# Cross-attention logits as eight 32-channel products in one set, with ScalarE's other work gathered between tiles

## The chip, the cores and the metric

The kernel runs on one core of one Trainium2 chip. Its engines work side by side, each through its own list of instructions in order, and wait for one another on semaphores: TensorE (matrix products, PE in the rows), VectorE (DVE), ScalarE (ACT), GpSimd (POOL) and SyncE, which only starts transfers. The metric is the device time of one execution in microseconds (us); for the kernel before it is the median of three runs.

## The reference

A decoder layer on x of 4 sequences x 1024 tokens x 256 channels and a context of 4 x 77 x 256. Three blocks follow each other, each with a residual and a layer norm over the channels:

```
x = layernorm(x + self_attention(x))      # one head, sigmoid weights
x = layernorm(x + cross_attention(ctx, x))
x = layernorm(x + time_mixing(x))
```

The middle one is what the change is in. With 16 heads of 16 channels:

```
qh = split_heads(q @ wq_w.T + wq_b)       # q is x
kh = split_heads(k @ wk_w.T + wk_b)       # k, v are the context, 77 rows
vh = split_heads(v @ wv_w.T + wv_b)
logits = jnp.einsum('bhqd,bhkd->bhqk', qh, kh) * scale
attn = jax.nn.softmax(logits, axis=-1)
out = jnp.einsum('bhqk,bhkd->bhqd', attn, vh)
return merge_heads(out) @ dense_w.T + dense_b
```

## The kernel before

The 4096 tokens are 32 tiles of 128, taken in pairs: NJ = 16 pairs, pair i holding tiles 2i and 2i+1. Each engine's program is written out by hand as a list of calls in Python, and that list is the order in which it works; a call waits for the semaphores of the work that it needs (`w.wait_ge`). Self-attention fills the first 300 us. Then comes the loop `for s in range(NJ)`, sixteen steps of cross-attention, and after it the time mixing, which begins with `mixes(0)` on VectorE.

A tile's way in the loop, with the names of the calls and of what they write:

1. `x1` (TensorE) transposes the normed tokens of a pair; `x1_hi` (ScalarE) and `x1_lo` (VectorE) split them into a high and a low part; `query` (TensorE) makes the queries, and ScalarE's `query` copies them to `xq` with the bias. Channels lie on the 128 partitions, in two halves e = 0, 1 of 128 channels (8 heads each).
2. `cross_scores(t, e)` (TensorE, L1303) makes the logits of 8 heads of tile t. The keys lie in `kb` as blocks: in the 64 partitions of four heads, four blocks of 77 columns, each zero but in the rows of its own head. One product over 64 partitions with 308 columns so gives four heads at once, and two such products, of the upper and the lower 64 partitions, make the half set e. They are plain float32, which TensorE does in two passes, each with its weight load. The four results of a tile go to four banks of PSUM (`big` and `ring` in the rows). A half set waits until the exponentials of the same half of tile t-1 are read out.
3. `maxima(t, e)` (VectorE, L906, `neg_mx`) takes the minima of the negated logits, per bank; `exponentials(t, e)` (ScalarE, L400, `p_sb`) then makes the softmax numerators, one instruction per head, four per bank.
4. `fold_weights(t)` (GpSimd, L658, `fold`) adds the two halves of each head's 78 columns, `sums(t)` (VectorE, L912, `sm`) and `reciprocals(t)` (L919, `rc`) make the reciprocal sums, `normalise(t)` (GpSimd, L663) multiplies them in. `fold` is one buffer, `sm` and `rc` are two.
5. `weights_t(t, c)` (TensorE, L1319) turns the weights, in three parts c; `weights_body` (VectorE, L926, `pT`) copies two of them out of PSUM, `weights_tail` (ScalarE) the third.
6. `mixed(i)` (TensorE, L1336) multiplies with the values for a pair, 32 columns of the array at a time; `mixed_hi` (ScalarE) and `mixed_lo` (VectorE, `oT_lo`) split the result; `dense(i)` is the output product; `crossed(i)` (VectorE, L939) adds the residual, `stats2` (L944, L949), `deviation2` (GpSimd) and `norm2` (ScalarE) are the layer norm.

Steps overlap: step s makes the logits of pair s, turns the weights of tiles 2s-3 and 2s-2, mixes pair s-2, does the dense product of pair s-3 and the norm of pair s-4. GpSimd's list in a step is `fold_weights(2s-1)`, `residual2(s)`, `normalise(2s-1)`, `fold_weights(2s)`, `normalise(2s)`, `deviation2(s-3)`. On VectorE `sums(2s)` is nearly the last of the step, and the ordering of the calls around it is what the rows and lists below show.

Ahead of the loop the first half set of tile 0 is written before the last `attend` of self-attention, and `maxima(0, 0)` before `attended(NG - 1)`, which frees the banks of the second half.

## Time and profile before

| | us |
|---|---|
| median of 3 runs | 595.7 (595.64 to 595.77) |
| the profiled execution | 593.07 |
| its span, first to last instruction | 591.1 |
| TensorE busy in the span | 544.1 (92%) |
| VectorE busy | 439.9 (74%) |
| ScalarE busy | 377.5 (64%) |
| GpSimd busy | 339.1 (57%) |
| exponentials (L400) out of `big`, 384 | 89.8, 359 ns each |
| logits' products (L1303) into `big`, 192 passes | 51.1, 482 ns each |

The times of the runs are of whole executions, the span is that of the instructions alone. Busy times are sums of durations, and the matmuls' ends are modelled: where they are pipelined, durations overlap, so that what a product costs is read from the starts of it and of the next. The granted clock of TensorE was 0.985 of 2.4 GHz over the span, and 1.00 in each 20 us from 340 to 480 us. A row of the timeline merges like instructions in a row (x4: four of them); the number in brackets is the time in which the engine had nothing to do before them, and behind the arrow is what ended it.

### The profile page before, as it was taken

The page shows a single profiled execution, that of the slowest core. Times are in us where ns is not written, and L with a number is a line of the kernel's source. Part 1 is how long each engine was busy: PE and PEld are TensorE (multiplying, and loading weights), DVE is VectorE, ACT ScalarE, POOL GpSimd, SP SyncE. Part 2 cuts the span into 40 slices and gives each one's busy share as a digit, 9 for nine tenths or more (in the row PEclk, how much of TensorE's full clock was granted, in tenths as well). Part 3 has the DMA queues.
Part 4 walks back from the last instruction along what each step waited for, and adds up shares of the span by engine and source line. Part 5 has one row for each costly group of instructions (what it writes and reads, how often), then busy time and mean ns, then how long its engine had stood idle before and what let it go on. Part 6 is the DMA issues. An engine that isn't in the chain of part 4 may idle for free.

```text
span 591.1 us, 11142 instructions
## 1 busy us (share of the span) xinstructions
PE 544.1 (92%) x3952; PEld 453.6 (77%) x3952; DVE 439.9 (74%) x1027; ACT 377.5 (64%) x1013; POOL 339.1 (57%) x382
## 2 busy tenths in 40 slices
PE   3879999999999999999978999999999986899993
PEld 2668988898998989987765677667767655799993
DVE  2975577666666777666537889889989878799995
ACT  1254344444344454443368989999899885899974
POOL 2645245253435334150427887898898883169996
PEclk9999999999999999999988999999999998999997
DMA  6210101010103002110000000000000000001113
GB/s 182 71 55 19 54 19 54 19 53 19 41 21 101 1 1 72 34 54 2 0 2 0 2 2 2 0 3 1 1 3 1 2 2 0 1 19 55 54 54 108
DMA packets 18351, 17.53 MB, mean 30 GB/s; under 512 B 1835, under 2 KB 18296, under 8 KB 18296
## 3 DMA queue, kind: packets, MB, share of 16 engines
q1 hardware_dynamic: 18024, 16.57, 9.1%
q8 instruction: 31, 0.51, 0.4%
q10 hardware_dynamic: 272, 0.26, 0.1%
q14 instruction: 24, 0.20, 0.1%
HBM read 12.63 MB, written 4.19 MB: 28 GB/s over the span
## 4 chain that ended last, share of the span: by engine, by line
PE 47%; POOL 20%; DVE 16%; ACT 8%; issue 6%; DMA 2%; SPq 1%; POOLq 0%; DVEq 0%; ACTq 0%
PE ring L218 20%; PE big L218 19%; POOL p_sb L663 9%; POOL fold L658 6%; DVE big L970 3%; ACT p_sb L400 2%; POOL xs L650 2%; PE ring L1209 2%; PE big L1303 2%; POOL rs L674 1%; DVE xmT_lo L788 1%; PE ring L1319 1%; DVE y L996 1%; DMA bo<-in_bo 1%; DVE st L817 1%
## 5 line engine op out<-in xcount | busy, mean ns | idle before, releaser
L788 DVE TENSOR_TENSOR aT_lo<-a_sb,aT_hi 128x512 fp32r<-128x512 f32 x64 | 45.8, 717 | 78.2 <-ACT aT_hi L324 78.2
L400 ACT ACTIVATE p_sb<-big,neg_mx 128x77 f32<-128x77 f32 x384 | 89.8, 359 | 13.3 <-DVE neg_mx L906 13.2
L663 POOL TENSOR_TENSOR p_sb<-p_sb,rc 128x1248 f32<-128x1248 f32 x32 | 72.8, 2277 | 23.3 <-DVE rc L919 23.3
L218 PE MATMUL big<-vv_hi,aT_hi 128*128 128x256 f32 x256 | 72.7, 284 | 4.0 <-DVE xs L852 4.0
L357 ACT ACTIVATE a_sb<-ring,nlogs 128x512 f32<-128x512 f32 x64 | 43.5, 680 | 49.5 <-PE ring L218 49.5
L218 PE MATMUL big<-vv_hi,aT_lo 128*128 128x256 f32 x256 | 72.5, 283 | 0.0
L218 PE MATMUL big<-vv_lo,aT_hi 128*128 128x256 f32 x256 | 72.4, 283 | 0.0
L1319 PE MATMUL ring<-ident,p_sb 128*128 128x128 f32 (+1 forms) x384 | 55.5, 280 | 8.4 <-DVE pT L926 7.8
L1319 PEld LDWEIGHTS ring<-ident,p_sb 128*128 128x128 f32 (+1 forms) x384 | 40.2, 130 | 29.3 <-issue 20.5
L1303 PE MATMUL big<-kb,xq 64*128 64x308 f32 x192 | 51.1, 482 | 5.9 <-ACT p_sb L400 4.5
L218 PEld LDWEIGHTS big<-vv_hi,aT_hi 128*128 128x128 f32 x256 | 48.8, 191 | 9.1 <-issue 6.8
L218 PE MATMUL ring<-qkT_hi 128*128 128x512 f32 x128 | 51.6, 403 | 0.0
L218 PEld LDWEIGHTS big<-vv_lo,aT_hi 128*128 128x128 f32 x256 | 48.8, 191 | 2.1
L587 POOL TENSOR_TENSOR rs<-mv,consts 128x2 f32<-128x2 f32 x32 | 12.5, 389 | 65.9 <-DVE mv L820 65.9
L218 PE MATMUL ring<-qkT_lo,qkT_hi 128*128 128x512 f32 x128 | 50.2, 392 | 0.0
L658 POOL TENSOR_TENSOR fold<-p_sb 128x624 f32<-128x624 f32 x32 | 48.7, 1523 | 2.3 <-ACT p_sb L400 2.3
L218 PE MATMUL ring<-qkT_hi,qkT_lo 128*128 128x512 f32 x128 | 49.9, 390 | 0.0
L218 PEld LDWEIGHTS big<-vv_hi,aT_lo 128*128 128x128 f32 x256 | 48.8, 191 | 0.0
L324 ACT ACTIVATE xT_hi<-xraw 128x512 fp32r<-128x512 f32 x16 | 10.1, 630 | 56.2 <-PE big L218 50.0
L906 DVE TENSOR_REDUCE neg_mx<-big 128x4 f32<-128x308 f32 x96 | 41.3, 459 | 4.9 <-PE big L1303 3.6
L926 DVE COPY pT<-ring 128x512 f32<-128x512 f32 x64 | 43.3, 680 | 1.7 <-PE ring L1319 1.7
L597 POOL TENSOR_TENSOR vv_lo<-v_sb,vv_hi 128x512 fp32r<-128x512 f32 x16 | 21.0, 1315 | 40.5 <-ACT vv_hi L324 40.5
(172 smaller groups left out, 1748.8 us busy)
## 6 DMA issues: line engine op xcount, KB each, us to landing
xraw<-in_xT SPq DMA_DIRECT2D x16, 256.0 KB, 2.8
xs<-in_x SPq DMA_DIRECT2D x8, 512.0 KB, 3.8
out_y<-y SPq DMA_DIRECT2D x16, 256.0 KB, 2.1
cT<-in_cT SPq DMA_DIRECT2D x1, 308.0 KB
wraw<-in_wqT ACTq DMA_DIRECT2D x1, 256.0 KB, 3.9
wraw<-in_wkT SPq DMA_DIRECT2D x1, 256.0 KB, 4.3
wv_raw<-in_wv SPq DMA_DIRECT2D x1, 256.0 KB, 5.7
wo_ls<-in_woT SPq DMA_DIRECT2D x1, 256.0 KB, 5.8
```

Of the source, the lines that this page charges most:

```text
L218: mm = pe.matmul(out, s_, m_, start=first and k == 0 and q == 0, stop=last and k == n - 1 and q == 2, skip_group_check=not check)
L357: act.activation(a_sb[:, i % NAR], st_bank[i % 2], ACT.Sigmoid, bias=nlogs[:, 0:1], scale=1.0 / 16).then_inc(st_act.sem, 1)
L400: ex = act.activation(weights(t)[:, HG * g + h, 0:SC], logits[g][:, h * SC:(h + 1) * SC], ACT.Exp, bias=neg_mx[:, t % 2, HG * g + h:HG * g ...
L597: pool.tensor_tensor(lo, tiles(v_sb[:, i % 2]), f(hi), ALU.subtract).then_inc(v_pool.sem, 1)
L658: pool.tensor_tensor(fold[:].rearrange("p (h k) -> p h k", k=FO), p[:, :, 0:FO], p[:, :, FO:2 * FO], ALU.add).then_inc(fo_pool.sem, 1)
L663: pool.tensor_tensor(weights(t), weights(t), rc[:, t % 2].rearrange("p (h o) -> p h o", o=1) .to_broadcast([P, H, SP]), ALU.mult).then_inc ...
L788: return dve.tensor_tensor(lo, whole, f(hi), ALU.subtract)
L906: dve.tensor_reduce(neg_mx[:, t % 2, HG * g:HG * (g + 1)], logits[g][:, 0:LW].rearrange("p (h k) -> p h k", k=SC), AX, ALU.min)\
L926: dve.tensor_copy(pT[:, t // 2 % 2, c, :, (t % 2) * P:(t % 2 + 1) * P], tiles(tp_bank[(3 * t + c) % 2], NH)).then_inc(tp_dve.sem, 1)
L970: dve.scalar_tensor_tensor(out=xm_bank[m][:, k * D:(k + 1) * D], in0=ty_bank(i)[:, k * D:(k + 1) * D], scalar=mu[:, m, k:k + 1], in1=carry ...
L1303: mm = pe.matmul(logits[2 * e + r][:, 0:LW], xq[half, i % 2, e * D + u * P:e * D + (u + 1) * P], kb[half, b, e], start=True, stop=True)
L1319: mm = pe.transpose(tp_bank[n % 2][0:rows, g * P:(g + 1) * P], p_sb[:, t % NP, c0:c0 + rows], ident[:])
```

## The change

The keys' blocks get smaller: two heads in the 32 partitions of two heads (KH = 2, KW = 154 columns). `cross_scores(t)` makes all sixteen heads of a tile in one set: for each half e of the channels, four products over 32 partitions with 154 columns, into the four banks, each bank getting two heads of either half. The set waits for all exponentials of tile t-1. `maxima(t)` and `exponentials(t)` do all four banks of a tile in a row. The first half set ahead of the last `attend` goes. The lists of ScalarE, VectorE and TensorE are written anew, with the other calls between the tiles. `query(s + 2)` at the end of a step becomes `query(s + 1)` in its middle.

The diff, cut:

```diff
@@ -29,6 +29,8 @@
+KH = 2
+KW = KH * SC
@@ -143,11 +146,11 @@
-            mask_k = tensor(ph, "mask_k", [P, HG])
+            mask_k = tensor(ph, "mask_k", [P, KH])
-            kb = tensor(ph, "kb", [P, B, KC, LW])
+            kb = tensor(ph, "kb", [P, B, KC, KW])
@@ -381,7 +384,7 @@
                 def query(i):
                     w.wait_ge(*xq_pe.at(i))
                     if i >= 2:
-                        w.wait_ge(*xs_pe.at(2 * (2 * (i - 2) + 1) + 1))
+                        w.wait_ge(*xs_pe.at(2 * (i - 2) + 1))
                     for e in range(KC):
                         cut = slice(e * D, (e + 1) * D)
                         copy(xq[:, i % 2, cut], x_bank[:, cut], bias=bqcol[:, e:e + 1]).then_inc(xq_act.sem, 1)
@@ -389,16 +392,17 @@
                 def first_exponential():
                     act.activation(spare[:], minus4[:, 0:1], ACT.Exp).then_inc(table.sem, 1)
-                def exponentials(t, e):
+                def exponentials(t):
                     if t >= NP:
                         w.wait_ge(*tp_pe.at(3 * (t - NP) + 2))
                     else:
                         w.wait_ge(*st_pe.at(NS - 1))
-                    for g in (2 * e, 2 * e + 1):
-                        w.wait_ge(*mx_dve.at(4 * t + g))
+                    for n in range(4):
+                        w.wait_ge(*mx_dve.at(4 * t + n))
                         for h in range(HG):
-                            ex = act.activation(weights(t)[:, HG * g + h, 0:SC], logits[g][:, h * SC:(h + 1) * SC], ACT.Exp,
-                                                bias=neg_mx[:, t % 2, HG * g + h:HG * g + h + 1], scale=-1.0)
+                            ex = act.activation(weights(t)[:, h // KH * (H // 2) + KH * n + h % KH, 0:SC],
+                                                logits[n][:, h * SC:(h + 1) * SC], ACT.Exp,
+                                                bias=neg_mx[:, t % 2, HG * n + h:HG * n + h + 1], scale=-1.0)
                         ex.then_inc(ex_act.sem, 1)
                 def weights_tail(t):
@@ -415,9 +419,9 @@
-                def norm2(i):
+                def norm2(i, ts=(0, 1)):
-                    for t in range(2):
+                    for t in ts:
@@ -516,24 +520,24 @@
                 first_exponential()
                 x1_hi(2)
                 for s in range(NJ):
-                    exponentials(2 * s, 0)
+                    exponentials(2 * s)
                     if s >= 2:
                         weights_tail(2 * s - 3)
-                    exponentials(2 * s, 1)
-                    if s and s + 2 < NJ:
-                        x1_hi(s + 2)
+                    if s and s + 1 < NJ:
+                        query(s + 1)
                     if s == 1:
                         norm1_last()
                     if s >= 4:
-                        norm2(s - 4)
-                    exponentials(2 * s + 1, 0)
+                        norm2(s - 4, (0,))
+                    exponentials(2 * s + 1)
+                    if s and s + 2 < NJ:
+                        x1_hi(s + 2)
                     if s >= 2:
                         mixed_hi(s - 2)
-                    exponentials(2 * s + 1, 1)
+                    if s >= 4:
+                        norm2(s - 4, (1,))
                     if s >= 1:
                         weights_tail(2 * s - 2)
-                    if s + 2 < NJ:
-                        query(s + 2)
                 first_sigmoid()
                 weights_tail(NT - 3)
                 carried(0)
@@ -640,9 +644,9 @@
-                                           .to_broadcast([P, HG, SC]),
+                                           .to_broadcast([P, KH, SC]),
-                                           .to_broadcast([P, HG, SC]), ALU.mult).then_inc(kb_pool.sem, 1)
+                                           .to_broadcast([P, KH, SC]), ALU.mult).then_inc(kb_pool.sem, 1)
@@ -898,13 +902,13 @@
                     w.wait_ge(*tx_act.at(i))
                     low_part(*hi_lo(x1T, i % 2), x_bank).then_inc(tx_dve.sem, 1)
-                def maxima(t, e):
-                    w.wait_ge(*xs_pe.at(2 * t + e))
+                def maxima(t):
+                    w.wait_ge(*xs_pe.at(t))
                     if t >= 2:
                         w.wait_ge(*ex_act.at(4 * (t - 2) + 3))
-                    for g in (2 * e, 2 * e + 1):
-                        dve.tensor_reduce(neg_mx[:, t % 2, HG * g:HG * (g + 1)],
-                                          logits[g][:, 0:LW].rearrange("p (h k) -> p h k", k=SC), AX, ALU.min)\
+                    for n in range(4):
+                        dve.tensor_reduce(neg_mx[:, t % 2, HG * n:HG * (n + 1)],
+                                          logits[n][:, 0:LW].rearrange("p (h k) -> p h k", k=SC), AX, ALU.min)\
                             .then_inc(mx_dve.sem, 1)
                 def sums(t):
@@ -1087,37 +1091,30 @@
                         value_blocks(4)
                         value_blocks(5)
                 x1_lo(2)
-                maxima(0, 0)
                 attended(NG - 1)
-                maxima(0, 1)
                 for s in range(NJ):
-                    if s:
-                        maxima(2 * s, 0)
+                    maxima(2 * s)
                     if s >= 2:
                         weights_body(2 * s - 3, 0)
+                        weights_body(2 * s - 3, 1)
                     if s >= 3:
                         crossed(s - 3)
-                    if s:
-                        maxima(2 * s, 1)
-                    if s >= 2:
-                        weights_body(2 * s - 3, 1)
                     if s >= 1:
                         sums(2 * s - 1)
                         reciprocals(2 * s - 1)
-                    maxima(2 * s + 1, 0)
+                    maxima(2 * s + 1)
+                    if s == 0:
+                        stats1(NG - 1)
                     if s >= 1:
                         weights_body(2 * s - 2, 0)
+                    sums(2 * s)
+                    reciprocals(2 * s)
+                    if s >= 1:
+                        weights_body(2 * s - 2, 1)
                     if s and s + 2 < NJ:
                         x1_lo(s + 2)
-                    maxima(2 * s + 1, 1)
-                    if s == 0:
-                        stats1(NG - 1)
                     if s >= 2:
                         mixed_lo(s - 2)
-                    if s >= 1:
-                        weights_body(2 * s - 2, 1)
-                    sums(2 * s)
-                    reciprocals(2 * s)
                     if s >= 3:
                         stats2(s - 3)
                 weights_body(NT - 3, 0)
@@ -1287,21 +1284,21 @@
                                            [hi_lo(x1T, i % 2, slice(k * D, (k + 1) * D)) for k in range(KC)])
                     mm.then_inc(xq_pe.sem, 1)
-                def cross_scores(t, e):
+                def cross_scores(t):
                     i, u = divmod(t, 2)
                     b = t // TB
                     w.wait_ge(*xq_act.at(i))
                     w.wait_ge(*kb_pool.at(b))
                     if t:
-                        w.wait_ge(*ex_act.at(4 * (t - 1) + 2 * e + 1))
-                    elif e:
+                        w.wait_ge(*ex_act.at(4 * (t - 1) + 3))
+                    else:
+                        w.wait_ge(*vb_dve.at(5))
                         w.wait_ge(*ln1a_dve.at(NG - 1))
-                    else:
-                        w.wait_ge(*vb_dve.at(5))
-                    for r in range(2):
-                        half = slice(64 * r, 64 * (r + 1))
-                        mm = pe.matmul(logits[2 * e + r][:, 0:LW], xq[half, i % 2, e * D + u * P:e * D + (u + 1) * P],
-                                       kb[half, b, e], start=True, stop=True)
+                    for e in range(KC):
+                        for n in range(4):
+                            own = slice(32 * n, 32 * (n + 1))
+                            mm = pe.matmul(logits[n][:, e * KW:(e + 1) * KW], xq[own, i % 2, e * D + u * P:e * D + (u + 1) * P],
+                                           kb[own, b, e], start=True, stop=True)
                     mm.then_inc(xs_pe.sem, 1)
                 def weights_t(t, c):
@@ -1451,32 +1448,28 @@
                 attend(NS - 3)
                 attend(NS - 2)
                 x1(2)
-                cross_scores(0, 0)
                 attend(NS - 1)
                 for s in range(NJ):
-                    if s:
-                        cross_scores(2 * s, 0)
+                    cross_scores(2 * s)
+                    if s >= 2:
+                        weights_t(2 * s - 3, 0)
+                        weights_t(2 * s - 3, 1)
                     if s >= 3:
                         dense(s - 3)
+                    if s and s + 1 < NJ:
+                        query(s + 1)
                     if s >= 2:
-                        weights_t(2 * s - 3, 0)
-                    cross_scores(2 * s, 1)
+                        weights_t(2 * s - 3, 2)
+                    cross_scores(2 * s + 1)
+                    if s >= 1:
+                        weights_t(2 * s - 2, 0)
+                        weights_t(2 * s - 2, 1)
                     if s >= 2:
-                        weights_t(2 * s - 3, 1)
-                        weights_t(2 * s - 3, 2)
+                        mixed(s - 2)
                     if s and s + 2 < NJ:
                         x1(s + 2)
-                    cross_scores(2 * s + 1, 0)
                     if s >= 1:
-                        weights_t(2 * s - 2, 0)
-                    if s >= 2:
-                        mixed(s - 2)
-                    cross_scores(2 * s + 1, 1)
-                    if s >= 1:
-                        weights_t(2 * s - 2, 1)
                         weights_t(2 * s - 2, 2)
-                    if s + 2 < NJ:
-                        query(s + 2)
                 dense(NJ - 3)
                 for c in range(3):
                     weights_t(NT - 3, c)
@@ -1505,7 +1498,7 @@
     row = np.arange(P)
-    mask_k = ((row[:, None] // DH) % HG == np.arange(HG)[None, :]).astype(np.float32) * np.float32(-DH ** -0.5)
+    mask_k = ((row[:, None] // DH) % KH == np.arange(KH)[None, :]).astype(np.float32) * np.float32(-DH ** -0.5)
     flat = np.arange(3 * P)
     sel = ((flat[None, :] % SP == np.arange(SC)[:, None]) & (flat[None, :] < PG)).astype(np.float32)
     head = flat.reshape(3, P).T // SP
```

VectorE's list around `sums(2s)` in a middle step, before (`x1T_lo` is `x1_lo`, `oT_lo` is `mixed_lo`, `pT` are the copies of `weights_body`, `sm` the sums; the first row is `weights_body(2s-2, 0)`):

```order
L926 COPY pT<-ring 128x4x128
L788 TENSOR_TENSOR x1T_lo<-ring,x1T_hi 128x512
L906 TENSOR_REDUCE neg_mx<-big 128x4 x2
L788 TENSOR_TENSOR oT_lo<-ring,oT_hi 128x512
L926 COPY pT<-ring 128x4x128
L912 TENSOR_REDUCE sm<-fold 128x16
L919 RECIPROCAL rc<-sm 128x16
L944 BN_STATS st<-xs 128x6 x2
L949 BN_AGGR mv<-st 128x2 x2
```

And now:

```order
L930 COPY pT<-ring 128x4x128
L916 TENSOR_REDUCE sm<-fold 128x16
L923 RECIPROCAL rc<-sm 128x16
L930 COPY pT<-ring 128x4x128
L792 TENSOR_TENSOR x1T_lo<-ring,x1T_hi 128x512
L792 TENSOR_TENSOR oT_lo<-ring,oT_hi 128x512
L948 BN_STATS st<-xs 128x6 x2
L953 BN_AGGR mv<-st 128x2 x2
```

The low part of x1, that of the mixed values and the second copy have moved from ahead of the sums of tile 2s to behind their reciprocal. The minima of tile 2s+1 are all ahead of the first copy now.

ScalarE's list over one step, before (`p_sb` are exponentials, eight heads of a half in the first two rows):

```order
L400 ACTIVATE p_sb<-big,neg_mx 128x77 x4
L400 ACTIVATE p_sb<-ring,neg_mx 128x77 x4
L324 ACTIVATE pT<-ring 56x4x128
L400 ACTIVATE p_sb<-big,neg_mx 128x77 x8
L324 ACTIVATE x1T_hi<-ring 128x512
L324 ACTIVATE xs<-xs,nb,rs 128x256 x2
L400 ACTIVATE p_sb<-big,neg_mx 128x77 x4
L400 ACTIVATE p_sb<-ring,neg_mx 128x77 x4
L324 ACTIVATE oT_hi<-ring 128x512
L400 ACTIVATE p_sb<-big,neg_mx 128x77 x8
```

And now:

```order
L403 ACTIVATE p_sb<-big,neg_mx 128x77 x4
L403 ACTIVATE p_sb<-ring,neg_mx 128x77 x4
L403 ACTIVATE p_sb<-big,neg_mx 128x77 x8
L327 ACTIVATE pT<-ring 56x4x128
L327 ACTIVATE xq<-ring,bqcol 128x256 x2
L327 ACTIVATE xs<-xs,nb,rs 128x256
L403 ACTIVATE p_sb<-big,neg_mx 128x77 x4
L403 ACTIVATE p_sb<-ring,neg_mx 128x77 x4
L403 ACTIVATE p_sb<-big,neg_mx 128x77 x8
L327 ACTIVATE x1T_hi<-ring 128x512
L327 ACTIVATE oT_hi<-ring 128x512
```

Sixteen exponentials stand in a row now, and the copies of the weights' tail, the queries, x1 and the mixed values and the halves of `norm2` (`xs`) are behind them.

## Rows read from the trace of the kernel before

**Rows 1.** Timelines at the ends of the stage: start us, us, engine, line, operation

```profile
310.27 1.39 DVE L857 BATCH_NORM_STATS2 stl<-xs 128x6 f32<-128x256 f32 x4
...
313.57 2.27 POOL L663 TENSOR_TENSOR p_sb<-p_sb,rc 128x1248 f32<-128x1248 f32 x1
...
344.81 2.28 POOL L663 TENSOR_TENSOR p_sb<-p_sb,rc 128x1248 f32<-128x1248 f32 x1 [1.72 <-DVE rc L919]
...
479.71 0.39 PE L218 MATMUL ring<-wx_hi,oT_hi 128*128 128x256 f32 x1 [1.11 <-DVE oT_lo L788]
...
481.33 2.28 POOL L663 TENSOR_TENSOR p_sb<-p_sb,rc 128x1248 f32<-128x1248 f32 x1 [1.25 <-DVE rc L919]
...
488.80 1.67 DVE L970 SCALAR_TENSOR_TENSOR big<-ring,mu,carry 128x256 f32<-128x256 f32 x4
```

**Rows 2.** Waits of all engines, 360 to 460 us: total us, times, longest

```profile
POOL p_sb L663 <- DVE rc L919: 12.5, 9, 1.5
...
DVE sm L912 <- POOL fold L658: 8.5, 9, 1.0
...
ACT p_sb L400 <- DVE neg_mx L906: 5.3, 8, 0.7
```

**Rows 3.** Timeline of TensorE, one step

```profile
400.47 0.28 PE L218 MATMUL ring<-x1T_hi,wx_lo 128*128 128x256 f32 x1
400.68 0.52 PE L1303 MATMUL big<-kb,xq 64*128 64x308 f32 x1
...
401.04 0.42 PE L1303 MATMUL big<-kb,xq 64*128 64x308 f32 x1
...
401.39 0.39 PE L218 MATMUL ring<-wx_hi,oT_hi 128*128 128x256 f32 x1
...
407.08 1.93 PE L1336 MATMUL ring<-pT,vb 128*32 128x256 f32 x32
```

**Rows 4.** Timeline of TensorE, two half sets in a row

```profile
305.44 0.42 PE L1303 MATMUL ring<-kb,xq 64*128 64x308 f32 x1
...
305.70 0.42 PE L1303 MATMUL ring<-kb,xq 64*128 64x308 f32 x1
```

**Rows 5.** Timeline of ScalarE, the same step

```profile
399.75 1.84 ACT L400 ACTIVATE p_sb<-big,neg_mx 128x77 f32<-128x77 f32 x8
401.41 0.67 ACT L324 ACTIVATE pT<-ring 56x512 f32<-56x512 f32 x1
```

**Rows 6.** Timeline of VectorE, the same step

```profile
401.15 0.79 DVE L912 TENSOR_REDUCE sm<-fold 128x16 f32<-128x624 f32 x1
401.98 0.25 DVE L919 RECIPROCAL rc<-sm 128x16 f32<-128x16 f32 x1
402.15 0.69 DVE L944 BATCH_NORM_STATS2 st<-xs 128x6 f32<-128x256 f32 x2
...
402.97 0.46 DVE L906 TENSOR_REDUCE neg_mx<-big 128x4 f32<-128x308 f32 x1
...
403.73 0.68 DVE L926 COPY pT<-ring 128x512 f32<-128x512 f32 x1
404.33 0.68 DVE L939 TENSOR_TENSOR xs<-ring,xs 128x512 f32<-128x512 f32 x1
404.93 0.85 DVE L906 TENSOR_REDUCE neg_mx<-big 128x4 f32<-128x308 f32 x2
...
407.32 0.80 DVE L912 TENSOR_REDUCE sm<-fold 128x16 f32<-128x624 f32 x1 [0.95 <-POOL fold L658]
```

**Rows 7.** Timeline of GpSimd, the same step

```profile
402.31 2.28 POOL L663 TENSOR_TENSOR p_sb<-p_sb,rc 128x1248 f32<-128x1248 f32 x1 [1.48 <-DVE rc L919]
...
405.78 1.51 POOL L658 TENSOR_TENSOR fold<-p_sb 128x624 f32<-128x624 f32 x1
...
408.50 2.27 POOL L663 TENSOR_TENSOR p_sb<-p_sb,rc 128x1248 f32<-128x1248 f32 x1
410.73 1.53 POOL L658 TENSOR_TENSOR fold<-p_sb 128x624 f32<-128x624 f32 x1
```

More of the change, by code:

```diff
@@ L1295, in cross_scores @@
                     if t:
-                        w.wait_ge(*ex_act.at(4 * (t - 1) + 2 * e + 1))
-                    elif e:
-                        w.wait_ge(*ln1a_dve.at(NG - 1))
+                        w.wait_ge(*ex_act.at(4 * (t - 1) + 3))
                     else:
                         w.wait_ge(*vb_dve.at(5))
-                    for r in range(2):
-                        half = slice(64 * r, 64 * (r + 1))
-                        mm = pe.matmul(logits[2 * e + r][:, 0:LW], xq[half, i % 2, e * D + u * P:e * D + (u + 1) * P],
-                                       kb[half, b, e], start=True, stop=True)
+                        w.wait_ge(*ln1a_dve.at(NG - 1))
+                    for e in range(KC):
[3 more added lines that the diff above has]
+                                           kb[own, b, e], start=True, stop=True)
                     mm.then_inc(xs_pe.sem, 1)
```

## The prediction

> **What bounds the kernel now.** I read the views in this order: the page's busy shares, the waits of the cross-attention steps, the timelines of one step on each engine, and the rows at its two ends. The kernel has three parts: self-attention to 301 us, sixteen steps of cross-attention (two tiles of 128 tokens a step) to about 481 us, and the mixing behind it. Only the middle one is changed, so its step is the thing to price. The normalising product on GpSimd at step 3 starts at 344.81 and at step 15 at 481.33 [rows 1]: 12 steps in 136.52 us, 11.38 us a step.
>
> Over 100 us of it TensorE shows no wait for another engine; GpSimd waits 12.5 us for VectorE's reciprocals, VectorE 8.5 us for GpSimd's folds, ScalarE 5.3 us for the minima [rows 2]. So TensorE sets the step, but narrowly: ScalarE, idle for 5% of it, has some 10.8 us of work in 11.38, and VectorE and GpSimd wait for each other. A TensorE that is relieved can give back 0.6 us a step at most, and only if the other loops turn faster than 11.38.
>
> **Price of the products on TensorE.** A half set now (two 64-row products, two passes each) starts 0.21 us behind the multiply before it, where a plain multiply takes 0.12: 0.09 of drain. Its passes start at 400.68 and 401.04, the next work at 401.39, so 0.36 and 0.35 us [rows 3]. Where two half sets follow each other the spacing is 0.26 (305.44 to 305.70) [rows 4]; so a pass streams 308 columns in 0.26, and only the first load (0.10) and the drain (0.09) lie open. With the first load of the work behind, also open (0.10), a half set costs 0.09+0.36+0.35+0.10 = 0.90 us, and a step has four: 3.6.
>
> The new set has eight products of 154 columns, two passes each: 16 multiplies in four groups of four. A group streams for 0.26/2 = 0.13 if its four run together. The trace has no four row groups together, but it has four column groups: 32 multiplies of 256 columns took 1.93 us [rows 3], where one by one they would take 32 x 0.26 x 256/308 = 6.9. So I take four together: 0.09+0.10+4x0.13+0.09+0.10 = 0.90 for the set. The lower bound is 0.7, if switching costs nothing; the upper is one by one, 16 x 0.13 + 0.38 = 2.5. TensorE then has two sets instead of four half sets, 1.8 us less a step, about 9.5 us of work.
>
> The Trainium skill, TensorE: Matmul & The Clock Gate, Part 3 (packing small matmuls), says that a weight load overlaps a running multiply only where their row groups differ. By that rule each group would show its load, and the set would take 4x0.23+0.28 = 1.2 us, an estimate. The trace disagrees: the same row groups follow at 0.26, with no load between [rows 4].
>
> **The loop over the logits.** With one set, the products of a tile wait for all sixteen exponentials of the tile before. Eight exponentials take 399.75 to 401.41 [rows 5], 0.21 each, so 3.32 for sixteen; then about 0.2 until the last is written, 0.8 for the set and 0.5 for the first minimum: 4.8 us a tile, 9.6 a step. What waits there is ScalarE's exponentials, and the copies of earlier tiles gathered behind them fill most of that time. With 10.8 us of work ScalarE stays under 11.38 too. With the set at 2.5 us this loop is 6.5 a tile, 13 a step, and decides.
>
> **The loop over VectorE and GpSimd.** Here the order matters. Three pieces of VectorE's step used to stand ahead of the sums of tile 2s (the low part of x1, the low part of the mixed values, the second copy of the turned weights), and hid the fold that the sums wait for. Now they stand behind the sums. The way from the sums of tile 2s-1 to those of 2s leads over GpSimd, where the fold of 2s stands behind the normalising of 2s-1. Step by step, start to start [rows 6, 7]:
> sums 2s-1 0.83 (401.15 to 401.98); reciprocal to normalising 0.33 (401.98 to 402.31); normalising 2.23 (408.50 to 410.73); fold until the sums start 1.54 (405.78 to 407.32); sums 2s 0.83; reciprocal 0.17; then the copy, x1's low part and the mixed low part, three of 128x512 out of PSUM at 0.60 (403.73 to 404.33); statistics 0.82 (402.15 to 402.97); four minima 1.52 (402.97 to 403.73 for two); two copies and the residual sum 1.80. Together 11.87 us, and it closes on the sums of tile 2s+1. In the order before, the three pieces of 0.60 were not in it: 10.07 us, below TensorE's 11.38. Nothing in this loop is TensorE's, so its gain is worth nothing here: the stall moves from TensorE to VectorE, which is late by 0.5 us a step. For ScalarE I cost the new places at nothing: norm2 in two parts and the query's copy stand in the time between tiles, where it would wait; without that cover they are the same instructions and come to the same 10.8 us.
>
> **The sum.** Steps 3 to 15: eleven links at 11.87 and the last, which has no x1, at 11.27: 141.84 against 136.52, +5.3. Steps 0 to 3 took 31.24 us (313.57 to 344.81), 10.4 a link: the first ones hang on GpSimd's own work and stay, the third lacks the statistics, 11.87-0.82 = 11.05, about as now; I take them at -0.2 together, an estimate. Start: the first tile is no longer half done ahead of the last attend. Its sixteen exponentials stand behind one another (+8x0.21 = 1.66), two more minima stand ahead of the first statistics (+0.76), and the attend comes 0.8 earlier since no half set is ahead of it: the statistics at 310.27 [rows 1] come 1.6 later, and the first normalising (313.57) with them. End: dense(13) starts at 479.71, held up by the mixed low part, and mixes(0) at 488.80 [rows 1], 9.1 later. That low part now stands behind the sums of tile 30 and the copy. Normalising at step 15 comes at 481.33+6.7 = 488.0, so the sums at 486.9, the copy at 487.9, the low part at 488.5 and dense at 489.2. From there 8.3 us (the 9.1 less the 0.8 in which the next low part stood behind the last sums): mixes(0) at 497.5, +8.7, of which 2.0 are the new exit. Everything behind hangs on mixes(0), and I carry the shift whole.
>
> Smaller changes: the block keys have half the columns, work of GpSimd hidden under self-attention, at nothing; one mask load is shorter. TensorE has gaps of at most 0.6 us in a step now, which I take as too short to lower its clock; it was granted in full all through these steps before.
>
> The profiled execution took 593.07 us for a span of 591.1; the three timed ones have a median of 595.7. The shift is a difference of schedules, so I add it to the median: 595.7 + 8.7 = 604.4 us.
>
> **The rivals.**
> First, the four don't run together, only two or one. For it: no row shows four row groups. Against it: four column groups do, and two row groups do now, or a pass of both would take 0.52 and not 0.26 [rows 4]. In pairs the set is 1.4 us, the logits loop 10.8, hidden still, with some +1 at the start. One by one (2.5 us) the logits loop of 13.0 a step decides: 12 x (13.0-11.38) = 19, with 2 at the start and 2 at the end 23: 618 us. Half-way prices give 608 to 615.
> Second, faster: the VectorE loop does not bind because its pieces are shorter together than start-to-start spacings say, or the folds come earlier. It decides if the loop falls by more than 0.5 us, to under 11.38. Then ScalarE's 10.8 us are the step: 12 x 0.6 = 7.2 less, 1.6 more at the start: 590 us. For it: TensorE's 1.8 us are real, and ScalarE's work is under 11.38. Against: each term of 11.87 is a row, and the engines run in order.
> Third, the two effects meet and the time stays at 595.7: a loop near 11.3, with start and end shifts given back. Nothing speaks for it but that errors can cancel.
> Fourth, the change doesn't do what it says on the logits: TensorE's wait for sixteen exponentials lengthens, as ScalarE's gathered copies wait in turn for TensorE (the copy of x1 and of the weights' tail are produced behind the products). That gives another 0.3 to 0.5 us a step, 609 us.
>
> **How the numbers follow.** Forecast (loop at 11.6 to 12.0, 601 to 607 us) 0.62. Products or copies slower (607 to 618) 0.19. Faster 0.12. No change 0.03, and a weak slow-down of 1 to 5 us 0.04. A change under 0.2%, 1.2 us, can't be told from none. Slower then is 0.62+0.19+0.04 = 0.85, the same 0.03, faster 0.12. For 8 in 10 the range has to hold the forecast and most of the slower cases: 598 to 611.
>
> **What the profile will show.** If right: GpSimd's normalising of tile 2s starts every 11.9 us; VectorE waits for a fold once a step, about 1.2 us, and not for the other; the gap of the logits' multiplies between groups is 0.13; TensorE waits some 2 us a step for exponentials and copies; the first normalising at 315.2. Wrong on the products: groups at 0.26 or more. Wrong on the loop: VectorE's copy behind the sums not followed at once, or steps under 11.4.

## The result and the profile after

The changed kernel took 605.8 us (median of four, 604.35 to 607.62) against 595.7 (595.13 to 595.77): 1.73% slower, ratio 1.0173 [1.0137, 1.0209]. The forecast was 604.4. The profiled execution of after took 607.07 us for a span of 604.8, so it is one of its longer ones: its span is 13.7 us over that of before (591.1), the medians lie 10.1 apart. What follows explains the 13.7 of the two profiled executions.

The rows below are from the changed kernel's timelines: GpSimd's normalising of tile 2s at steps 0, 3 and 15, and VectorE's mixes(0). Columns are start, duration, engine, line, operation, idle time before and what ended it:

```profile
315.54 2.27 POOL L667 TENSOR_TENSOR p_sb<-p_sb,rc 128x1248 f32<-128x1248 f32 x1
...
348.77 2.28 POOL L667 TENSOR_TENSOR p_sb<-p_sb,rc 128x1248 f32<-128x1248 f32 x1 [1.20 <-DVE rc L923]
...
490.87 2.28 POOL L667 TENSOR_TENSOR p_sb<-p_sb,rc 128x1248 f32<-128x1248 f32 x1 [1.21 <-DVE rc L923]
```
```profile
500.81 1.67 DVE L974 SCALAR_TENSOR_TENSOR big<-ring,mu,carry 128x256 f32<-128x256 f32 x4
```

Against [rows 1] that is +1.97 at the start, +2.0 in steps 0 to 3 (33.23 against 31.24), +5.6 in steps 3 to 15 (142.10 against 136.52, eleven links of 11.89 and one of 11.29), +2.5 from there to mixes(0) (9.94 against 7.47), and +1.7 behind it (104.0 against 102.3 to the end of the span).

The longest waits between 360 and 460 us (engine and line, what it waits for, total, times, longest):

```profile
POOL p_sb L667 <- DVE rc L923: 13.4, 17, 1.2
ACT p_sb L403 <- DVE neg_mx L910: 12.6, 9, 1.4
PE big L1300 <- ACT p_sb L403: 11.1, 17, 1.1
DVE sm L916 <- POOL fold L662: 9.5, 9, 1.1
```

In [rows 2] TensorE waited for nobody. Now it waits for the exponentials before every set (17 times in 8.4 steps), ScalarE's waits have more than doubled (5.3 to 12.6) and VectorE waits for one fold a step, 1.1 us. Everybody waits for somebody: a closed way through several engines, a loop, sets the step. Its course is on the chain of waits, one step from 402 us (start, duration, what; most rows left out):

```profile
402.95 0.29 issue
...
403.27 2.28 POOL p_sb L667
405.55 1.48 POOL fold L662
...
407.06 0.82 DVE sm L916
...
408.15 0.54 DVE pT L930
408.69 0.59 DVE x1T_lo L792
409.29 0.60 DVE oT_lo L792
409.88 0.39 DVE st L948 x2
...
411.19 0.66 POOL rs L678
...
412.12 1.49 POOL fold L662
413.61 1.23 POOL xs L654
```

The first half is the loop of the forecast: normalising, fold, sums, and behind the sums the three pieces that used to hide the fold. Behind the statistics the forecast went on over VectorE (minima, copies, sums); the chain goes over GpSimd's deviation, fold and residual instead. That branch is 0.29 us shorter than mine: for so long GpSimd stands ready for the normalising (the first row) until the reciprocals are there. The timelines show what the normalising really waits for:

```profile
402.12 0.79 DVE L916 TENSOR_REDUCE sm<-fold 128x16 f32<-128x624 f32 x1
...
402.94 0.25 DVE L923 RECIPROCAL rc<-sm 128x16 f32<-128x16 f32 x1
...
403.27 2.28 POOL L667 TENSOR_TENSOR p_sb<-p_sb,rc 128x1248 f32<-128x1248 f32 x1 [0.33 <-DVE rc L923]
```

From the sums at 407.06 to the reciprocals of the next step VectorE has no hole, so in the changed kernel the branch over VectorE ends last, as forecast.

The set of products, on TensorE's timeline:

```profile
402.91 0.39 PE L1300 MATMUL big<-kb,xq 32*128 32x154 f32 x1 [1.03 <-ACT p_sb L403]
...
403.15 0.29 PE L1300 MATMUL ring<-kb,xq 32*128 32x154 f32 x1
...
403.41 0.29 PE L1300 MATMUL ring<-kb,xq 32*128 32x154 f32 x1
...
403.64 1.09 PE L1316 MATMUL ring<-ident,p_sb 128*128 128x128 f32 x8
```

Four groups of four (the third starts at 403.28), 0.24 and then 0.13 apart: the four products do run together, and 154 columns take half of the 0.26 of [rows 4]. From its first product to the next work the set takes 0.73 us. My 0.90 also holds 0.09 of drain ahead of the set, which here lies in the wait, and 0.10 for the first load of the next work; between the same two starts it has 0.10+0.52+0.09 = 0.71. So the price was right within 0.02. The weight loads of the second group start at 403.01, in the same four row groups that multiply from 402.91 on. The Trainium skill (TensorE: Matmul & The Clock Gate, Part 3) states that a load overlaps a running product only where their row groups differ; with this the trace again disagrees. The same section of the Trainium skill also lets a load go ahead of running products when it goes to a background weight buffer, which would allow what the trace shows; no run here shows the buffer itself.

TensorE's clock, by stretches (length, busy time of PE, PEld, DVE, ACT, POOL, granted clock, DMA). After:

```profile
300.00:320.00 20.00, 8.93 (x84) 7.63 (x82) 10.07 (x26) 11.31 (x51) 9.43 (x13) 0.74 0.00 0
320.00:340.00 20.00, 16.05 (x164) 12.93 (x165) 14.40 (x31) 17.27 (x65) 16.09 (x10) 0.83 0.01 2
340.00:480.00 140.00, 118.98 (x1378) 92.33 (x1376) 119.48 (x270) 123.72 (x477) 115.62 (x104) 1.00 0.01 2
...
500.00:520.00 20.00, 14.30 (x109) 12.61 (x110) 14.13 (x33) 11.27 (x24) 2.92 (x11) 0.83 0.00 1
```

And before:

```profile
300.00:320.00 20.00, 14.51 (x80) 9.70 (x79) 12.02 (x31) 14.62 (x58) 11.39 (x14) 0.83 0.00 0
320.00:340.00 20.00, 19.25 (x168) 13.38 (x170) 16.68 (x36) 18.53 (x77) 16.66 (x11) 1.00 0.01 2
...
500.00:520.00 20.00, 18.06 (x162) 16.22 (x162) 14.02 (x30) 18.05 (x41) 2.85 (x8) 1.00 0.00 1
```

In the steady steps the clock is full in both, as forecast. At the ends it is lower than before: 0.74 against 0.83 in the first stretch, 0.83 against 1.00 in the second and behind 500 us. Ahead of the second and third set TensorE waits 4.2 us for sixteen exponentials, and those sets run at the lower of the two levels, 1.2 GHz (granted clock 0.50, groups 0.25 apart):

```profile
309.21 0.62 PE L1300 MATMUL big<-kb,xq 32*128 32x154 f32 x1 [4.19 <-ACT p_sb L403]
...
314.81 0.62 PE L1300 MATMUL big<-kb,xq 32*128 32x154 f32 x1 [4.20 <-ACT p_sb L403]
```

### The profile page after: what moved, and what is told of

Its sections match the earlier page's. It is cut to its first block, busy times and chain, and to the rows that moved or that the text cites. A ratio compares the mean times of both kernels' runs of the same rounds, so it can differ in the third digit from the quotient of the medians.

```text
span 604.8 us, 11640 instructions
## 1 busy us (share of the span) xinstructions
PE 528.4 (87%) x4208; PEld 455.6 (75%) x4208; DVE 440.4 (73%) x1027; ACT 376.7 (62%) x1013; POOL 338.2 (56%) x382
## 4 chain that ended last, share of the span: by engine, by line
PE 43%; DVE 23%; POOL 19%; ACT 6%; issue 5%; DMA 2%; SPq 1%; POOLq 0%; DVEq 0%; ACTq 0%
PE big L221 18%; PE ring L221 18%; POOL fold L662 7%; POOL p_sb L667 6%; DVE big L974 3%; POOL xs L654 3%; PE ring L1206 2%; ACT p_sb L403 2%; DVE sm L916 2%; DVE oT_lo L792 1%; DVE pT L930 1%; DVE xmT_lo L792 1%; DVE y L1000 1%; DMA bo<-in_bo 1%; POOL rs L678 1%
## 5 line engine op out<-in xcount | busy, mean ns | idle before, releaser
L403 ACT ACTIVATE p_sb<-big,neg_mx 128x77 f32<-128x77 f32 x384 | 92.1, 390 | 28.5 <-DVE neg_mx L910 28.5
L1316 PE MATMUL ring<-ident,p_sb 128*128 128x128 f32 (+1 forms) x384 | 58.9, 287 | 12.3 <-DVE pT L930 7.6
L1316 PEld LDWEIGHTS ring<-ident,p_sb 128*128 128x128 f32 (+1 forms) x384 | 41.9, 134 | 23.3 <-DVE pT L930 8.8
L1300 PE MATMUL big<-kb,xq 32*128 32x154 f32 x384 | 28.3, 338 | 31.7 <-ACT p_sb L403 30.2
L1300 PEld LDWEIGHTS big<-kb,xq 32*128 32x128 f32 x384 | 20.4, 201 | 40.1 <-ACT p_sb L403 35.3
L327 ACT ACTIVATE xT_hi<-xraw 128x512 fp32r<-128x512 f32 x16 | 10.1, 630 | 55.7 <-PE big L221 50.0
```

Source lines behind the costliest of these rows:

```text
L403: ex = act.activation(weights(t)[:, h // KH * (H // 2) + KH * n + h % KH, 0:SC], logits[n][:, h * SC:(h + 1) * SC], ACT.Exp, bias=neg_mx[: ...
L1300: mm = pe.matmul(logits[n][:, e * KW:(e + 1) * KW], xq[own, i % 2, e * D + u * P:e * D + (u + 1) * P], kb[own, b, e], start=True, stop=True)
L1316: mm = pe.transpose(tp_bank[n % 2][0:rows, g * P:(g + 1) * P], p_sb[:, t % NP, c0:c0 + rows], ident[:])
```

## The experiments

Every ratio is to the kernel before on the same chip, in the same rounds (its medians there were 593 to 595). "Step" is the spacing of GpSimd's normalising in the steady part, 11.89 in the changed kernel. A time that is read from a single trace also holds what came before the loop: the first set starts at 304.21 in the changed kernel, but at 305.81 in experiment 1, 306.08 in 6, 304.00 in 3 and 303.77 to 304.04 in 5, 7, 8 and 9, though none of their edits touches the self-attention ahead of it.

**1. One term out of the loop.** On VectorE, `stats2(s - 3)` goes from the end of the step to its middle:

```
+                    if s >= 3:
+                        stats2(s - 3)
                     maxima(2 * s + 1)
...
                     if s >= 2:
                         mixed_lo(s - 2)
-                    if s >= 3:
-                        stats2(s - 3)
```

> The changed kernel with one call moved on VectorE: the statistics of pair s-3 stand ahead of the minima of tile 2s+1, where VectorE waits 0.6 us for the products anyway, and no longer between the sums of tile 2s and those of 2s+1. Theory A (the loop over VectorE and GpSimd, 11.87 us, sets the step): the loop loses the 0.82 us of the statistics and is 11.05, so steps of 11.05 to 11.2 us, 12 of them, and some 9 us less than the changed kernel: about 597. Rival B (the loop over the logits, with its wait for sixteen exponentials on TensorE, sets the step): nothing changes, 605 to 606, steps of 11.9.

Measured: step 11.17, ratio 1.0055 [1.0038, 1.0073], 597.5 us. Moving 0.82 us of work, without removing any, gives back two thirds of the slow-down (1.18 of 1.73%). So the step is set by something that goes through VectorE's statistics, as the forecast's loop does; experiment 5 shows a second loop that also does. What decides next is GpSimd's own chain, whose only hole is a wait for reciprocals:

```profile
400.42 2.28 POOL p_sb L667
402.69 1.48 POOL fold L662
404.18 1.17 issue
...
405.38 2.28 POOL p_sb L667
```

**2. Wide products in the new order.** Each set as four products of 64 channels again (and the exponentials' heads in the order that goes with them):

```
-KH = 2
+KH = HG
...
-                        for n in range(4):
-                            own = slice(32 * n, 32 * (n + 1))
-                            mm = pe.matmul(logits[n][:, e * KW:(e + 1) * KW], xq[own, i % 2, e * D + u * P:e * D + (u + 1) * P],
-                                           kb[own, b, e], start=True, stop=True)
+                        for r in range(2):
+                            half = slice(64 * r, 64 * (r + 1))
+                            mm = pe.matmul(logits[2 * e + r][:, 0:LW], xq[half, i % 2, e * D + u * P:e * D + (u + 1) * P],
+                                           kb[half, b, e], start=True, stop=True)
```

> The schedule of the changed kernel with the products of before: four of 64 partitions and 308 columns in the one set of a tile. A set then takes about 0.10+4x0.26+0.18 = 1.3 us on TensorE in place of 0.8. Theory A: TensorE has slack in every step of the new schedule, the step stays at 11.9, only the first steps, where each tile waits for its products, get longer: +1 to +2 us over the changed kernel, 607. Rival B (TensorE or the logits loop sets the step): 32 sets x 0.5 = +16 us, 621.

Measured: step 12.15, ratio 1.0310 [1.0288, 1.0332], 613.2 us: between the two. In this order the narrow products save 0.26 a step, not 1: 3.1 us of the 7.4 between the medians. By the traces another 1.5 lie in the first normalising (317.02), 0.9 in steps 0 to 3 and 1.0 in the exit. The chain of a steady step tells why it is so little: it is now a loop over the logits, and it goes through VectorE's pieces, which my 9.6 us for that loop had left out:

```profile
400.35 0.69 DVE x1T_lo L792
...
402.43 0.47 DVE neg_mx L910
...
402.93 2.81 ACT p_sb L403 x13
...
406.54 0.52 PE big L1300
...
407.90 0.49 DVE neg_mx L910
```

**3. The clock of the first steps.** 28 products of 128x256 that nobody reads, behind each of the first two sets:

```
                     cross_scores(2 * s)
+                    if s == 0:
+                        keep_warm(28)
```

> The changed kernel with 28 products of 128x256 without a reader behind each of the first two sets of logits, on TensorE, which waits 4.2 us there (3.3 us of filling at the full clock). Theory C (the part of the slow-down that the forecast missed is the halved clock at 308 to 318 and 325 to 332 us): these stretches go, the first three steps take 31 us and not 33.2, and the time falls by 2 to 3 us, to 603; the spread between runs gets smaller. Rival D (the early steps are longer for the order of work): no change, or a little longer where the filling delays a set.

Measured: ratio 1.0156 [1.0133, 1.0180], 603.2 us; steps 0 to 3 took 32.71 (33.23 in after), the first normalising 314.72 (315.54), so the normalising of tile 30 comes 1.4 us earlier (489.50) and mixes(0) 1.5 (499.33). Of this 0.2 lies ahead of the first set (304.00 against 304.21), before any filler; the fillers' own part is 1.2 to 1.3. By the ratios the gain is 0.17%, 1.0 us, with intervals that overlap; the 2.5 us between the two medians come partly from a chip on which the kernel before is faster too. So the direction of C holds in the trace, and its size is 1 to 1.5 us rather than 2 to 3; steps 0 to 3 did not fall to its 31 us, and the runs are not closer together (602.4 to 605.8). The clock is held where the fillers run, and falls later instead:

```profile
300.00:320.00 20.00, 14.68 (x157) 13.25 (x155) 10.61 (x28) 12.51 (x54) 10.25 (x14) 1.00 0.00 1
320.00:340.00 20.00, 17.50 (x160) 14.10 (x159) 15.14 (x32) 17.13 (x68) 16.66 (x10) 0.74 0.01 2
```

**4. The three pieces back ahead of the sums,** the order of before on VectorE with everything else as changed:

```
                     if s >= 1:
                         weights_body(2 * s - 2, 0)
-                    sums(2 * s)
-                    reciprocals(2 * s)
-                    if s >= 1:
-                        weights_body(2 * s - 2, 1)
                     if s and s + 2 < NJ:
                         x1_lo(s + 2)
                     if s >= 2:
                         mixed_lo(s - 2)
+                    if s >= 1:
+                        weights_body(2 * s - 2, 1)
+                    sums(2 * s)
+                    reciprocals(2 * s)
```

> The changed kernel with VectorE's three pieces (low part of x1, low part of the mixed values, second copy of the turned weights) put back ahead of the sums of tile 2s, as in the kernel before. The plain reading of the forecast (these three behind the sums cost 0.5 us a step): the step falls to about 11.4 and the time to 600. Rival E: ScalarE makes the high parts only behind the sixteen exponentials of tile 2s+1 now, so VectorE would wait for them ahead of the sums and hold up the sums, the normalising and the next turned weights: steps of 13.4 us, 620 to 627 us. Then the move of the three pieces was forced by the gathering on ScalarE, and the cost is that of the two together.

Measured: step 13.5 to 13.6, ratio 1.0553 [1.0532, 1.0574], 627.0 us. With ScalarE's copies gathered behind the exponentials, VectorE stands in front of a copy that isn't there:

```profile
POOL p_sb L667 <- DVE rc L923: 25.5, 7, 3.7
DVE x1T_lo L792 <- ACT x1T_hi L327: 19.4, 8, 2.5
```

So with ScalarE's copies where they now are, VectorE can't keep its old order: the move that made the loop of 11.89 can't be undone alone.

**5. The other term out of the loop.** On GpSimd, the fold of 2s ahead of the normalising of 2s-1:

```
                         residual2(s)
-                        normalise(2 * s - 1)
                     fold_weights(2 * s)
+                    if s >= 1:
+                        normalise(2 * s - 1)
```

> The changed kernel with GpSimd's fold of tile 2s ahead of the normalising of tile 2s-1 and not behind it; VectorE's order untouched. Theory A (the step of 11.87 us is the loop sums - reciprocal - normalising - fold - sums): the normalising, 2.2 to 2.3 us, and its 0.33 us of wait leave the loop, which falls to about 9.6 us and no longer decides; the step is then that of the next loop, 11.4 to 11.6 us (the loop over the deviations ran 0.3 us under mine). The first normalising comes 1.2 us or so earlier behind the fold. Time 599 to 602 us. Rival B (GpSimd's sum of work or the order of VectorE alone decides, the place of the fold is nothing): steps of 11.9, time 605 to 607. Rival F (the turned weights, which wait for the normalising, come 1.5 us later and become the new bound): steps over 12.2, time over 610.

Measured: step 11.64, ratio 1.0146 [1.0121, 1.0171], 603.0 us. The step is clear in the trace; the interval of the ratio overlaps that of the changed kernel. A's step and time were a little too short, and the first normalising did not come 1.2 earlier (315.26 against 315.54, of which 0.26 lies ahead of the first set); that of tile 30 came 3.65 us earlier (487.22). 2.6 us left the loop and the step fell by 0.25: behind it stands a loop over ScalarE and VectorE, which was only 0.25 shorter than the first in the changed kernel:

```profile
403.13 2.78 ACT p_sb L403 x14
...
407.03 0.69 DVE x1T_lo L793
407.72 0.60 DVE oT_lo L793
408.32 0.39 DVE st L949 x2
...
409.11 0.47 DVE neg_mx L911
```

The statistics lie in this loop too, so experiment 1 shortened both and can't tell them apart. Experiment 5 can: the normalising that it took out, 2.23 us and a wait of 0.33, is in the forecast's loop and not in this one.

**6. Both** (edits 1 and 5 together).

> The fold first as in the kernel before this one, and the statistics ahead of the second maxima as in e1_stats_early. Theory A: the two are different loops; the statistics cut mine to 11.1 us and left GpSimd's chain with 1.17 us of wait for the reciprocals as the bound at 11.17, and the fold in front takes that wait away: steps of 10.8 to 11.0, first normalising earlier by 1.2, time 592 to 595 us, at or just below the kernel before. Rival: TensorE or ScalarE (10.8 us of work) is reached first through the exponentials: steps stay at 11.2 to 11.4, time 597 to 600.

Measured: step 10.92, from the sixth on 11.11; ratio 1.0036 [1.0018, 1.0054], 595.2 us. By the traces better than either alone: from the normalising of tile 0 to that of tile 30 it takes 163.5 us (166.4 in 1, 172.0 in 5), so the edits act on different loops; by the ratios it is not clear of experiment 1. The step settled above the 11.0 of theory A. The chain there runs over ScalarE's query copy, its exponentials and copies, and TensorE's turns and its dense and query products: the rival's engines, at a lower price than it named.

**7. A new order on three engines.** Edit 5; on VectorE the sums of 2s-1 ahead of the residual sum, and the statistics ahead of the low parts; ScalarE:

```
                     exponentials(2 * s)
-                    if s >= 2:
-                        weights_tail(2 * s - 3)
                     if s and s + 1 < NJ:
                         query(s + 1)
+                    if s >= 2:
+                        weights_tail(2 * s - 3)
...
-                    if s >= 4:
-                        norm2(s - 4, (0,))
...
-                    if s >= 4:
-                        norm2(s - 4, (1,))
                     if s >= 1:
                         weights_tail(2 * s - 2)
+                    if s >= 4:
+                        norm2(s - 4)
```

> Fold first on GpSimd; on VectorE the sums of tile 2s-1 directly behind the copies of the turned weights, and the statistics directly behind the second copy, ahead of the low parts of x1 and of the mixed values; on ScalarE the query's copy first behind the exponentials of 2s, and the whole second norm behind the last copy of the step. TensorE's order stays. Theory A (the products are worth 1.8 us a step on TensorE and only the order of the other engines hides it): steps of 10.6 to 10.8 us, all engines within 5 per cent of each other, first normalising 1.2 us earlier, time 589 to 592 us, faster than both kernels. Rival: ScalarE's 10.8 us of work plus its waits for the minima, some 0.3 a tile, are the floor: steps 11.2 to 11.4 and time 595 to 599 us.

Measured: step 10.77, ratio 0.9971 [0.9954, 0.9989], 592.3 us: 0.3% faster than before, at the edge of what was expected. Of the 5.3 us won up to the normalising of tile 30 (476.08 against 481.33), 4.2 were lost again in the exit: mixes(0) at 487.71 against 488.80.

**8. The same with the fillers of 3.**

> As e7_reordered, with 28 products of 128x256 that nobody reads behind each of the first two sets on TensorE, where the changed kernel shows waits of over 4 us and a low clock behind them. Theory C (the low clock of the first steps costs 2 to 3 us, of which e3_warm gave back 2.5): 1.5 to 3 us under e7_reordered. Rival: in the new order the first steps don't hang on TensorE, and the time is that of e7_reordered within 0.5 us.

Measured: ratio 0.9946 [0.9928, 0.9964], 590.4 us, 1.9 under the last in the same rounds; mixes(0) at 486.69, 1.0 earlier, though the first set starts 0.3 later (304.04 against 303.77): 1.3 by the traces. The 2.5 that the expectation takes from experiment 3 was too high, as said there, and the lower end of C is what came.

**9. The exit.** Two turns of tile 29 ahead of the dense product, their copies ahead of the residual sum:

```
+                weights_t(NT - 3, 0)
+                weights_t(NT - 3, 1)
                 dense(NJ - 3)
-                for c in range(3):
-                    weights_t(NT - 3, c)
+                weights_t(NT - 3, 2)
```

> e8_reordered_warm with one more edit behind the sixteen steps: TensorE turns the first two pieces of tile 29's weights ahead of dense(13) and not behind it, and VectorE copies both ahead of the residual sum. In e8 mixes(0) starts at 486.69, 11 us behind the normalising of tile 30; TensorE is idle 1.95 us before dense(13) and VectorE 3.5 us behind the low part that it waits for. Theory X (the exit costs a late dense and the turns that stand behind it): dense(13) no later, the turns and their copies in that idle time, mixes(0) at 484.2 to 485.5, time 1 to 2.5 us under e8, ratio to the kernel before 0.991 to 0.993. Rival: mixes(0) hangs on mixed(14) through tile 29's last copy and ScalarE's table load only, and stays at 486.5 or so: time as e8.

Measured: mixes(0) at 484.38 (486.69 in 8), ratio 0.9910 [0.9879, 0.9942], 588.7 us. The 2.3 us are in the trace; the ratios differ by as much, but their intervals overlap. This is the fastest version: 0.9% under the kernel before, with the products of the change.

**10. Wide products in that version** (edit 2 on top of 9).

> e9_exit with the sets of before's shape: four products of 64 channels, two side by side, 308 columns a pass, in place of eight of 32 channels. It asks what the products by themselves are worth once the order doesn't hide them: in e7 the chain of a step is ScalarE's work and, once a step, one whole set and one minimum. Theory A: the wide set is 1.3 us and the narrow one 0.8, on that chain once or twice a step, so 0.5 to 1.0 us a step more, steps of 11.3 to 11.8 and 7 to 14 us in all. Rival: the products are hidden (as they nearly were in the changed kernel, where the wide ones cost 0.26 us a step): under 0.3 us a step, under 4 us in all.

Measured: step 11.26, ratio 1.0061 [1.0041, 1.0081], 598.0 us. From the chain of a step in 9 (the last exponentials of a tile, its next set, the first minimum):

```profile
404.63 2.31 ACT p_sb L403 x10
...
406.98 0.39 PE big L1299
...
407.85 0.49 DVE neg_mx L909
```

and the same place in 10:

```profile
408.57 2.30 ACT p_sb L403 x10
...
410.92 0.52 PE big L1299
...
412.28 0.49 DVE neg_mx L909
```

From the start of a set to the first minimum behind it 0.87 us pass in 9 (406.98 to 407.85) and 1.36 in 10 (410.92 to 412.28): 0.49, once a step, and the step is 0.48 longer. The two profiled executions are 9.0 us apart. Steps 3 to 15 make 6.1 of it, the first normalising 1.2 (315.80 against 314.65) and steps 0 to 3 0.4. The exit up to mixes(0) takes as long in both (9.1); behind mixes(0) 10 is 1.3 longer, with the granted clock at 0.85 between 500 and 520 (1.00 in 9).

## Why the prediction was right, and where it was not

**The loop** (11.87 a step, +5.3): 11.89 and +5.6. Its terms hold one by one too: the three pieces take 1.73 us for 1.80, the statistics 0.88 for 0.82, the minima 1.53 for 1.52. Experiments 1 and 5 each took one of its terms away and each made the step shorter, and what 5 took out is not in the loop that the statistics also lie in; this is shown. It closes over minima and copies on VectorE, as the forecast had it, by the row of the normalising (it waits for the reciprocals, and VectorE has no hole). But the branch over GpSimd's deviation ends only 0.3 us earlier, and no experiment separates the two.

**The products** (0.90 a set, four together): 0.73 between the starts for which the forecast's terms give 0.71. Right in mechanism and size, and off the path in the changed kernel.

**The logits loop** (9.6 a step): this step failed. I counted exponentials, set and minimum, twice, and took the copies between tiles as filling a wait. But VectorE's minima of the next tile stand behind x1's low part, which waits for ScalarE's copy, which stands behind the exponentials. With that the loop is 11.64 (experiment 5), 0.25 short of deciding. The number that was forecast survived only because the other loop was longer by 0.25; that is luck. The second rival, "faster", suffers from the same gap: it priced a shorter VectorE loop at ScalarE's 10.8, where other loops stood in between. In 1, where mine was cut by 0.8, the step stopped at 11.17 on GpSimd; in 5 it stopped at 11.64.

**Steps 0 to 3** (-0.2): +2.0. **The clock** ("gaps of at most 0.6 us"): wrong at the start, where the gaps are 4.2 us, and wrong in the size of a steady one (1.0 to 1.3), though there the clock stayed full. I had read the clock only in the steps with full queues. Experiment 3 gave 0.5 of the +2.0 back, and 0.6 of the start (0.8, less the 0.2 ahead of the first set); how much of the rest is clock and how much ScalarE's gathered work stays open, since the fillers moved the low stretch instead of removing it.

**The start** (+1.6): +1.97. The set that waits for the attend starts 0.6 earlier (304.21 against 304.81), not 0.8; the rest wasn't taken apart. **The exit** (+2.0): +2.5. The clock was 0.91 between 480 and 500 in both kernels, so it doesn't explain the 0.5 by itself. **"Carried whole":** 1.7 more behind mixes(0), where the clock is 0.83 between 500 and 520 against 1.00 before. What placed this second low stretch wasn't tested.

**ScalarE's new places at nothing:** true in the changed kernel's step, and yet they belong to the cause. Experiment 4 shows that with the gathering VectorE's old order costs 13.6 a step, and the new order made the loop. It is not the gathering by itself: experiment 7 keeps the exponentials gathered and the pieces behind the sums, and its step is 10.77.

**The sum.** In the profiled executions the misses add up one way: forecast +8.7, measured +13.7. The median of the timed runs moved 10.1. So 604.4 against 605.8 is closer than its terms are, and that closeness is luck: the profiled execution of the changed kernel is one of its longer ones, and that of the kernel before one of its shorter.

## What to carry to other kernels

Relieving the engine that bounds a step brought nothing here while the order on the others closed a longer loop. Before such a change, write down each closed way through two or three engines and add it up, with everything queued ahead of a waiting instruction in it. Here the steps of 11.89, 11.64, 11.17, 11.11 and 10.77 us each had another chain behind them. The same narrow products cost 1.7% in one order, and with another, with fillers and a mended exit, the kernel gains 0.9%. In that last version wide products cost 1.5% (1.0061 against 0.9910), so the gain needs the narrow ones. Whether the kernel before, in its own order, would gain from the fold in front or the mended exit alone wasn't run. When work is gathered on one engine, look at what stands directly behind its consumers on the next.

## What the runs showed of the hardware

Four products of 32 rows start together, and the next four follow 0.13 us behind them for 154 columns, half of the 0.26 that 308 columns take in pairs of 64 rows [rows 4]. Of the weight loads of a set only the first shows (0.24 to the second group). At the low clock the spacing is 0.25. Products that nobody reads held the granted clock at 1.00 through 20 us in which it had been 0.74; the next 20 us, behind them, showed 0.74 instead of 0.83. The stage still ended earlier, by 1.2 us counted from its first set in experiment 3 (1.3 in the order of experiment 8).
